# A two-feed-forward, one-attention layer on one core: three stages put into one block, attention's weights prepared beside the others

## The chip, the core and the metric

The kernel runs on one core of one Trainium2 chip. A core has TensorE (PE), VectorE (DVE), ScalarE (ACT), GpSimd (POOL) and SyncE (SP), each with its own instruction stream, tied together by semaphores, and 16 DMA engines. The metric is the device time of one launch in microseconds (us), the lower the better.

## The reference

`x` has shape 16 x 1024 x 256. The layer is a feed-forward with its weights and inputs quantized to 4 bits, a causal linear attention with 16 heads, and the same feed-forward once more. LayerNorm stands in front of each.

```python
def _L0_attn_ref(x, Wqkv, bqkv, Wout, bout, gamma, beta):
    qkv = x @ Wqkv.T + bqkv
    q, k, v = jnp.split(qkv, 3, axis=-1)            # 16 heads of 16
    q = (jax.nn.elu(q) + 1.0 + FEAT_EPS) / jnp.sqrt(jnp.asarray(E, q.dtype))
    k = jax.nn.elu(k) + 1.0 + FEAT_EPS
    kv_cumsum = jnp.cumsum(jnp.einsum('blhe,blhf->blhef', k, v), axis=1)
    num = jnp.einsum('blhe,blhef->blhf', q, kv_cumsum)
    den = jnp.einsum('blhe,blhe->blh', q, jnp.cumsum(k, axis=1))[..., None] + FEAT_EPS
    out = (num / den).reshape(B, L, D) @ Wout.T + bout
    return (out - mu) / jnp.sqrt(var + LN_EPS) * gamma + beta

def _L0_ffn_ref(x, w_gate, w_up, w_down):           # fp4_linear quantizes x and w by blocks of 16
    h = jax.nn.silu(fp4_linear(x, w_gate)) * fp4_linear(x, w_up)
    return fp4_linear(h, w_down)

x = x + 0.5 * _L0_ffn_ref(_layernorm(x, axis=-1), L0_ffn_w_gate, L0_ffn_w_up, L0_ffn_w_down)
x = x + _L0_attn_ref(_layernorm(x, axis=-1), L0_attn_Wqkv, ...)
x = x + 0.5 * _L0_ffn_ref(_layernorm(x, axis=-1), L0_ffn_w_gate, L0_ffn_w_up, L0_ffn_w_down)
```

## The kernel before

The input is cut into N = 128 tiles of 128 rows (partitions) by 256. All of them stay in on-chip memory, in `x_sb`, from the first load to the last store. The program is a row of five blocks, each of which every engine leaves before any engine enters the next: `prepare_ffn` (quantized weights, L141), `ffn` for half 0 (L306), `prepare_attention` (L1012), `attention` (L602), `ffn` for half 1.

Inside a stage each engine runs a `step(i)` of its own, called by `pipeline` (L85): some first steps written out, a hardware loop of 8 steps a turn (4 in attention), some last steps written out. Engines work on different tiles in one step: in the feed-forward, ScalarE normalizes tile i+5, GpSimd makes the two-part input `x_hl` of tile i+2 (L503, L507), SyncE turns it by a transposing DMA into `xT` (L403), TensorE multiplies tile i by gate and up (L577), VectorE makes `hx` (L429) and its block scales (L436 to L480), GpSimd makes `h_hl` of tile i-2 (L512, L513), SyncE turns it into `hT` (L409), TensorE multiplies tile i-4 by down (L587) and VectorE adds it to `x_sb` (L456, semaphore `added`). In attention the chain of a tile is: statistics (L757), `rstd` and `shift` on GpSimd (L833 to L857), `xn` and `x_hl` (L911 to L866), `xT` (L731), queries, keys and values (L946, L953), `expo` (L898, L900, then L784 on VectorE, semaphore `feat`), scores (L983, L798), states (L804, L807, L840, L780), numerator (L967, L973), `o` (L793), `oT` (L737), output projection into `ps_z` (L1005), its LayerNorm (L752 to L862, L766, semaphore `attn_added`).

The order on each engine is the order of the code. SyncE issues every DMA of the kernel: its queue holds the loads of x (L391, each of which waits for the one before it to land), both kinds of transposes and the stores. SyncE's `pipeline` in the feed-forward starts 14 steps ahead, so that the loads of tiles 0 to 12 stand in front of the first `xT`.

`prepare_attention` loads the weights, folds biases in, finds a power-of-two scale (`partition_all_reduce` on GpSimd, L1069), splits the weights into two 16-bit parts `qkvo_hi` and `qkvo_lo` on VectorE (L1139 to L1141) and turns them by 32 TensorE transposes (L1156) and ScalarE copies (L1169).

## Time and profile before

| | us |
|---|---|
| median of 3 runs | 2363.45 (2363.09 to 2365.65) |
| the profiled execution, its own time | 2364.28 |
| its span in the trace | 2362.6 |
| TensorE, VectorE busy | 2174.2 (92%), 2134.8 (90%) |
| ScalarE, GpSimd busy | 1857.8 (79%), 1970.0 (83%) |

A row of the view in order of time reads: start, length, engine, line, operation, what it writes and reads, and in brackets how long the engine sat idle before it and what ended that. "SPq" is SyncE issuing a DMA, not the transfer itself. "issue" means idle time that no other engine's work explains. PEclk is the share of full speed that TensorE's clock was granted: 1.00 stands for 2.4 GHz, 0.50 for 1.2 GHz.

### The profile page before, as it was taken

The numbers are of one execution on the slowest core, as the hardware profiler recorded it, in microseconds if no ns is written. First come the engines' busy times: TensorE is split into PE (matmuls) and PEld (weight loads), VectorE is DVE, ScalarE is ACT, GpSimd is POOL, SyncE is SP. The second block draws the span as 40 slices with busy tenths as digits, with TensorE's granted clock in tenths as the row PEclk, the third lists the DMA queues.
The fourth block names the chain that finished last, engine by engine and source line by source line (L and its number), as shares of the span: only waits on it lengthen the run. The fifth ranks groups of instructions, "written<-read, shape, count | busy, mean of one in ns | idle before, by whom it ended". The sixth has DMA issues, their size and how long they took to land. (4 is left out here: it accounts for less than half of the span.)

```text
span 2362.6 us, 84983 instructions
## 1 busy us (share of the span) xinstructions
PE 2174.2 (92%) x27394; PEld 1559.3 (66%) x27394; DVE 2134.8 (90%) x5243; ACT 1857.8 (79%) x3910; POOL 1970.0 (83%) x3237
## 2 busy tenths in 40 slices
PE   1499999999999469999999999996999999999998
PEld 1266666666666358898989898983556656656565
DVE  7499999999999649999999999996999999999997
ACT  2588888888888267888888888885888888888885
POOL 0499999999999358999999999995988998988996
PEclk9799999999999779999999999997999999999999
DMA  1265555555555313333333333331555555555555
GB/s 37 71 117 114 113 111 115 116 114 114 114 112 95 72 39 69 68 68 68 68 68 68 68 68 68 68 68 29 104 113 114 109 115 112 109 116 110 111 114 117
DMA packets 729026, 215.24 MB, mean 91 GB/s; under 512 B 660358, under 2 KB 728710, under 8 KB 728966
## 3 DMA queue, kind: packets, MB, share of 16 engines
q1 hardware_dynamic: 728966, 214.52, 44.6%
q8 instruction: 28, 0.46, 0.1%
q14 instruction: 32, 0.26, 0.0%
HBM read 20.38 MB, written 16.78 MB: 16 GB/s over the span
## 5 line engine op out<-in xcount | busy, mean ns | idle before, releaser
L577 PE MATMUL ffn_ps_gu<-wgu_hi,ffn_xT 128*128 128x512 f16 (+1 forms) x3072 | 737.4, 363 | 50.4 <-DMA ffn_xT<-ffn_x_hl 50.4
L577 PEld LDWEIGHTS ffn_ps_gu<-wgu_hi,ffn_xT 128*128 128x128 f16 x3072 | 300.4, 98 | 336.2 <-DMA ffn_xT<-ffn_x_hl 52.7
L577 PE MATMUL ffn_ps_gu<-wgu_lo,ffn_xT 128*128 128x512 f16 (+1 forms) x1536 | 431.3, 363 | 0.0
L531 ACT ACTIVATE ffn_quarter<-ffn_y,offsets 128x960 int16<-128x960 f32 (+2 forms) x264 | 282.7, 1071 | 186.6 <-DVE ffn_y L467 186.0
L587 PE MATMUL ffn_ps_down<-wd_hi,ffn_hT 128*128 128x256 f16 x2816 | 351.2, 274 | 24.2 <-DVE x_sb L456 15.9
L512 POOL TENSOR_TENSOR ffn_h_hl<-ffn_q,ffn_h_scale_hi 128x704 f16<-128x704 f16 x256 | 350.8, 1370 | 15.9 <-DVE ffn_h_scale_lo L473 13.2
L513 POOL TENSOR_TENSOR ffn_h_hl<-ffn_q,ffn_h_scale_lo 128x704 f16<-128x704 f16 x256 | 353.8, 1382 | 0.0
L436 DVE TENSOR_REDUCE ffn_per_block<-ffn_hx 128x60 f32<-128x960 f32 (+2 forms) x264 | 298.5, 1131 | 42.2 <-ACT ffn_hx L561 19.8
L587 PEld LDWEIGHTS ffn_ps_down<-wd_hi,ffn_hT 128*128 128x128 f16 x2816 | 264.8, 98 | 106.7 <-issue 35.2
L467 DVE TENSOR_TENSOR ffn_y<-ffn_hx,ffn_per_block 128x960 f32<-128x960 f32 (+2 forms) x264 | 295.2, 1118 | 0.0
L559 ACT ACTIVATE ffn_odd<-ffn_quarter,offsets 128x960 f16<-128x960 int16 (+2 forms) x264 | 278.6, 1055 | 0.0
L429 DVE SCALAR_TENSOR_TENSOR ffn_hx<-ffn_ps_gu,unscale,ffn_silu 128x704 f32<-128x704 f32 x256 | 243.4, 951 | 37.1 <-PE ffn_ps_gu L577 24.4
L577 PEld LDWEIGHTS ffn_ps_gu<-wgu_lo,ffn_xT 128*128 128x128 f16 x1536 | 150.3, 98 | 155.2 <-issue 1.8
L526 ACT ACTIVATE ffn_silu<-ffn_ps_gu,unscale 128x704 f32<-128x704 f32 x256 | 211.8, 828 | 36.0 <-PE ffn_ps_gu L577 36.0
L503 POOL TENSOR_TENSOR ffn_x_hl<-ffn_q,ffn_x_scale_hi 128x256 f16<-128x256 f16 x256 | 157.5, 615 | 82.1 <-POOL ffn_rstd L495 40.4
L587 PE MATMUL ffn_ps_down<-wd_lo,ffn_hT 128*128 128x256 f16 x1536 | 210.6, 274 | 0.0
L946 PE MATMUL attn_ps_qk<-attn_xT,attn_wqkv_hi 128*128 128x128 f16 x2048 | 180.3, 221 | 15.9 <-DMA attn_xT<-attn_x_hl 15.9
L495 POOL TENSOR_TENSOR ffn_rstd<-ffn_rstd,minus_half 128x1 f32<-128x1 f32 x256 | 168.2, 657 | 20.0
L507 POOL TENSOR_TENSOR ffn_x_hl<-ffn_q,ffn_x_scale_lo 128x256 f16<-128x256 f16 x256 | 159.9, 625 | 20.0
L587 PEld LDWEIGHTS ffn_ps_down<-wd_lo,ffn_hT 128*128 128x128 f16 x1536 | 150.5, 98 | 18.1
L798 DVE TENSOR_TENSOR attn_scores<-attn_ps_sc,attn_causal 128x1024 f32<-128x1024 f32 x128 | 155.5, 1215 | 0.1
L946 PEld LDWEIGHTS attn_ps_qk<-attn_xT,attn_wqkv_hi 128*128 128x128 f16 x2048 | 142.5, 98 | 17.6 <-issue 16.2
(202 smaller groups left out, 5375.4 us busy)
## 6 DMA issues: line engine op xcount, KB each, us to landing
attn_v_eo<-attn_v_nat SPq DMA_DIRECT2D x512, 34.0 KB, 1.9
x_sb<-in_L_attn_x SPq DMA_DIRECT2D x128, 128.0 KB, 2.3
out<-x_sb SPq DMA_DIRECT2D x128, 128.0 KB, 2.1
ffn_xT<-ffn_x_hl SPq DMA_TRANSPOSE x256, 2.4
ffn_hT<-ffn_h_hl SPq DMA_TRANSPOSE x256, 3.6
attn_xT<-attn_x_hl SPq DMA_TRANSPOSE x128
attn_oT<-attn_o_hl SPq DMA_TRANSPOSE x128, 2.4
raw_qkvo<-in_L_attn_Wqkv SPq DMA_DIRECT2D x1, 768.0 KB, 5.1
```

The lines of the kernel that those rows point to most:

```text
L429: nc.vector.scalar_tensor_tensor(hx[par][:, 0:INNER], ps_gu[par][:, INNER:2 * INNER], unscale[:, 1:2], silu[:], ALU.mult, ALU.mult).then_i ...
L436: nc.vector.tensor_reduce(amax[:, blocks_in(front)], blocks(hx[par][:, front]), AXX, ALU.max, apply_absolute_value=True).then_inc(S["amax" ...
L467: nc.vector.tensor_tensor(blocks(y[:, front]), blocks(hx[par][:, front]), over_block(inv[:, at], at.stop - at.start), ALU.mult).then_inc(S ...
L495: nc.gpsimd.tensor_tensor(rstd[oth][:], rstd[oth][:], minus_half[:], ALU.pow).then_inc(S["rstd"], 1)
L512: nc.gpsimd.tensor_tensor(blocks(h_hl[par][:, 0:INNER]), blocks(q[par][:, 0:INNER]), over_block(h_scale_hi[par][:], HB), ALU.mult)
L513: nc.gpsimd.tensor_tensor(blocks(h_hl[par][:, INNER:]), blocks(q[par][:, 0:INNER]), over_block(h_scale_lo[par][:], HB), ALU.mult).then_inc ...
L526: nc.scalar.activation(silu[:], ps_gu[par][:, 0:INNER], ACT.Silu, scale=unscale[:, 0:1]).then_inc(S["silu"], 1)
L531: nc.scalar.activation(quarter[:, back], y[:, back], ACT.Identity, bias=offsets[:, 0:1], scale=4.0 / HALF_MIN).then_inc(S["quarter"], 1)
L559: nc.scalar.activation(odd[:, back], quarter[:, back], ACT.Identity, bias=offsets[:, 1:2], scale=HALF_MIN / 4.0).then_inc(S["odd"], 1)
L577: last = nc.tensor.matmul(ps_gu[par][:, a:b], xT[par][:, c, :], w[:, k, a:b], start=(n == 0), stop=(n == len(terms) - 1))
L587: last = nc.tensor.matmul(ps_down[:, 0:D], hT[par][:, c, :], w[:, c, :], start=(n == 0), stop=(n == len(terms) - 1))
L946: last = nc.tensor.matmul(ps_qk[:, col, :], w[:, at], aT, start=(n == 0), stop=(n == len(terms) - 1))
```

## The change

The five blocks become one, and no engine waits for all others between stages. A new `stages` writes each engine's whole program: feed-forward 0's first steps and loop, then 8 turns in which the last 8 steps of feed-forward 0 alternate with the first 8 of attention, attention's loop, then 7 turns in which the last 7 steps of attention alternate with the first 7 of feed-forward 1.

```diff
+    for i in range(first, end):
+        step(eng, i, i % 2)
+
+
+def in_turns(eng, step, first, end, turn):
+
     with eng.Fori(first, end - turn + 1, turn) as i:
         for k in range(turn):
-            step(i + k, (first + k) % 2)
-    for i in range(end, n + behind):
-        step(i, i % 2)
+            step(eng, i + k, (first + k) % 2)
+
+
+def stages(eng, N, ffn_0, attn, ffn_1, ffn_ahead=6, between=None):
+
+    first, ahead = 6, 4
+
+    def loop_end(n_ahead, begin, turn):
+        return begin + (N - n_ahead - begin) // turn * turn
+
+    in_order(eng, ffn_0, -ffn_ahead, first)
+    if between:
+        between(eng)
+    in_turns(eng, ffn_0, first, loop_end(ffn_ahead, first, TURN), TURN)
+    in_order(eng, ffn_0, loop_end(ffn_ahead, first, TURN), N + first - 2 * ahead)
+    for k in range(2 * ahead):
+        ffn_0(eng, N + first - 2 * ahead + k, k % 2)
+        attn(eng, k - ahead, k % 2)
+    attn_end = loop_end(ahead, ahead, ATTN_TURN)
+    in_turns(eng, attn, ahead, attn_end, ATTN_TURN)
+    in_order(eng, attn, attn_end, N + ahead - 7)
+    for k in range(7):
+        attn(eng, N + ahead - 7 + k, (N + ahead - 7 + k) % 2)
+        ffn_1(eng, k - 6, k % 2)
+    in_order(eng, ffn_1, 1, first)
+    in_turns(eng, ffn_1, first, loop_end(6, first, TURN), TURN)
+    in_order(eng, ffn_1, loop_end(6, first, TURN), N + first)
 
 
 def macaron(nc, x, wqkv, bqkv, wout, bout, gamma, beta, wg, wu, wd, out):
```

Attention's weights are prepared right after the feed-forward's, before any stage. In their preparation GpSimd subtracts the last column and makes the low part, and both parts are turned by two transposing DMAs of SyncE between step 5 and the loop of feed-forward 0. The rows of V's weights and biases are loaded by 16 small DMAs in the order in which they are used. The turned weights lie as `w_hi`, `w_lo` of [128, 8, 2, 128], so the V and output matmuls read 256 columns as two pieces of 128.

```diff
+        def _(sp):
+            def weights_turned(sp):
+                of_ffn.turn(sp)
+                of_attn.turn(sp)
+
+            of_ffn.sync(sp)
+            of_attn.sync(sp)
+            stages(sp, N, of_ffn_0.sync, of_attn_steps.sync, of_ffn_1.sync, 14, weights_turned)
...
+            stages(pe, N, of_ffn_0.tensor, of_attn_steps.tensor, of_ffn_1.tensor)
+
+
+@dataclass
+class Programs:
+
+    sync: Callable = None
+    turn: Callable = None
+    vector: Callable = None
+    gpsimd: Callable = None
+    scalar: Callable = None
+    tensor: Callable = None
+    reduce: Callable = None
+
+
+def prepare_ffn(nc, sem, scratch, wg, wu, wd, wgu_hi, wgu_lo, wd_hi, wd_lo, unscale, ident, ident16, minus_half, eps, minus_one, offsets):
 
     NG = WT * XB
     ND = DC * HB
     with ExitStack() as scope:
-        def sb(name, shape, dt=F32):
...
+
+    def sync(sp):
+        sp.dma_start(raw[:, 0:2 * DC, :], wqkv[0:2 * D].rearrange("(t p) k -> p t k", p=P)).then_inc(loaded, 16)
+        sp.dma_start(raw[:, QT:, :], wout.rearrange("(t p) k -> p t k", p=P)).then_inc(loaded, 16)
+        sp.dma_start(bias[:, 0:2 * DC], bqkv[0:2 * D].rearrange("(t p) -> p t", p=P), allow_slow_non_contiguous=True).then_inc(loaded, 16)
+        for j in range(HEADS // 2):
+
+            pair_of = slice(2 * D + j * 2 * E, 2 * D + (j + 1) * 2 * E)
+            sp.dma_start(raw[j * E:(j + 1) * E, 2 * DC:QT, :], wqkv[pair_of].rearrange("(a e) k -> e a k", a=2)).then_inc(loaded, 16)
+            sp.dma_start(bias[j * E:(j + 1) * E, 2 * DC:QT], bqkv[pair_of].rearrange("(a e) -> e a", a=2), allow_slow_non_contiguous=True).then_inc(loaded, 16)
+        for j, v in enumerate((bout, gamma, beta)):
+            sp.dma_start(rows[:, j, :], v.unsqueeze(0).to_broadcast([P, D])).then_inc(loaded, 16)
+
+    def turn(sp):
+        sp.wait_ge(split, 1)
+        for part, dst in ((hi, A.w_hi), (lo, A.w_lo)):
+            sp.dma_start_transpose(dst[:].rearrange("p t c m -> p (t c) m"), part).then_inc(S["w_turned"], 16)
+        sp.wait_ge(S["w_turned"], 32)
...
+                                pattern=[[0, DC], [E, 2 * PAIRS]], channel_multiplier=-1).then_inc(diag_ready, 1)
+        nc.gpsimd.memset(keep[:].rearrange("p (b c) -> p b c", c=CH)[:, :, 0:1], 0.0).then_inc(done, 1)
+
+
+        pool.wait_ge(loaded, 16 * LOADS)
+        nc.gpsimd.tensor_tensor(raw[:, 0:QT, 0:D - 1], raw[:, 0:QT, 0:D - 1], raw[:, 0:QT, D - 1:D].to_broadcast([P, QT, D - 1]), ALU.subtract).then_inc(centred, 1)
+        pool.wait_ge(centred, 1)
+        nc.gpsimd.tensor_scalar(raw[:, 0:2 * DC, D - 1], bias[:, 0:2 * DC], 1.0, None, ALU.add).then_inc(with_bias, 1)
+        nc.gpsimd.tensor_scalar(raw[:, 2 * DC:QT, D - 1], bias[:, 2 * DC:QT], 0.0, None, ALU.add).then_inc(with_bias, 1)
+
+    def reduce(pool):
+        pool.wait_ge(top_ready, 1)
+        nc.gpsimd.partition_all_reduce(gtop, top, P, RMAX).then_inc(gtop_ready, 1)
+        pool.wait_ge(scaled, 1)
+        nc.gpsimd.tensor_tensor(lo, raw_all, hi, ALU.subtract).then_inc(split, 1)
```

All scratch of the preparations lies in tiles 38 and up of `x_sb`, and the three stages' buffers lie at addresses written by hand in one area that they share. Where the barrier kept a stage from overwriting the one before, there are now single waits at the first steps. In feed-forward 1:

```diff
+
+                if half == 1 and isinstance(tm, int) and tm == 0:
+                    for even_odd in ("_even", "_odd"):
+                        act.wait_ge(T["xT" + even_odd], N * 8)
+                if half == 0:
+                    act.wait_ge(x_loaded, (tm + 1) * 16)
+                else:
+                    act.wait_ge(attn_added, tm + 1)
...
+
+                if half == 1 and isinstance(tn, int) and tn < 2:
+                    act.wait_ge(T["v_done"], N)
+                    act.wait_ge(T["k_odd"], N + tn - 1)
+                ready(act, "shift", tn)
...
+
+                if half == 1 and isinstance(tg, int) and tg == 1:
+                    pe.wait_ge(T["kv_first"], N)
+                    pe.wait_ge(T["o_ready"], N)
...
+
+                if half == 1 and isinstance(td, int) and td == 0:
+                    pe.wait_ge(T["z_gamma"], N)
```

and in attention (`F` is the feed-forward's semaphores):

```diff
+                freed(dve, "mid", i, 1)
+                if isinstance(i, int) and i == 0:
+                    last_turned(dve, "hT")
...
+            if isinstance(i, int) and i == -2:
+
+                pool.wait_ge(F["q"], N + X_AHEAD)
+                for j in range(2):
+                    nc.gpsimd.memset(v_nat[j][:], 1.0).then_inc(set_up, 1)
+                    nc.gpsimd.memset(v_eo[j][:], 0.0).then_inc(set_up, 1)
+            if isinstance(i, int) and i == 1:
+                last_turned(pool, "hT")
+                nc.gpsimd.memset(before[0][:], 0.0).then_inc(set_up, 1)
+                pool.wait_ge(set_up, 5)
...
+                freed(act, "kv_done", i, 1)
+                if isinstance(i, int) and i == 0:
+                    act.wait_ge(F["h_split"], N)
...
+
+                if isinstance(tf, int) and tf == 0:
+                    act.wait_ge(S["consts"], CONSTS)
+                    act.wait_ge(F["q"], N + X_AHEAD)
...
+
+                if isinstance(tf, int) and tf == 0:
+                    pe.wait_ge(S["consts"], CONSTS)
+                    pe.wait_ge(S["w_turned"], 32)
+                    pe.wait_ge(F["h"], N)
+                turned(pe, "xT", tf, oth)
+                freed(pe, "feat", tf, 1)
...
+
+                if valid(i, N):
+                    ready(pe, "k_nat", i)
+                for n, (aT, w, k) in enumerate(terms):
+                    last = nc.tensor.matmul(ps_v.rearrange("p (t m) -> p t m", t=DC), aT, w[:, 2 * DC:QT, k], start=(n == 0), stop=(n == len(terms) - 1))
+                last.then_inc(S["v_done"], 1)
+            if valid(tn, N):
+
+                if isinstance(tn, int) and tn == 0:
+                    pe.wait_ge(F["added"], N)
```

How this moves instructions. SyncE at the start of the program; `x_sb` as a target of weights is scratch. Before, the x loads stood behind a barrier:

```order
L189 DMA x_sb<-in_L_ffn_w_down 128x2x704
L145 UNCONDITIONAL_BRANCH
L385 UNCONDITIONAL_BRANCH [waits barrier_Pool_Activation_PE_DVE_SP_release]
L391 DMA x_sb<-in_L_attn_x 128x256
L391 DMA x_sb<-in_L_attn_x 128x256 [waits x_loaded] x12
L403 DMA_TRANSPOSE ffn_xT<-ffn_x_hl 128x4x128 [waits ffn_x_split]
L391 DMA x_sb<-in_L_attn_x 128x256 [waits x_loaded]
```

Now they stand right behind the weights' own loads (rows 4 to 22 are loads of attention's weights and biases, of which the last two of the 16 small ones are shown):

```order
L1174 DMA x_sb<-in_L_attn_Wqkv 16x2x256
L1175 DMA x_sb<-in_L_attn_bqkv 16x2x1
L1177 DMA attn_rows<-in_L_attn_bout 128x256
L1177 DMA attn_rows<-in_L_attn_gamma 128x256
L1177 DMA attn_rows<-in_L_attn_beta 128x256
L495 DMA x_sb<-in_L_attn_x 128x256
L495 DMA x_sb<-in_L_attn_x 128x256 [waits x_loaded] x12
L507 DMA_TRANSPOSE ffn_xT_88<-ffn_x_hl_84 128x4x128 [waits ffn_x_split]
L495 DMA x_sb<-in_L_attn_x 128x256 [waits x_loaded]
```

The 13 x loads no longer wait for the preparation to end, and they still stand in front of the first transpose.

SyncE at the loop of feed-forward 0. Before:

```order
L391 DMA x_sb<-in_L_attn_x 128x256 [waits x_loaded]
L403 DMA_TRANSPOSE ffn_xT<-ffn_x_hl 128x4x128 [waits ffn_x_split,ffn_up_done]
L409 DMA_TRANSPOSE ffn_hT<-ffn_h_hl 128x11x128 [waits ffn_h_split,ffn_down_done]
L92 UNCONDITIONAL_BRANCH
L92 ISA
L391 ISA [waits x_loaded]
L391 DMA x_sb<-in_L_attn_x 128x256
```

Now:

```order
L495 DMA x_sb<-in_L_attn_x 128x256 [waits x_loaded]
L507 DMA_TRANSPOSE ffn_xT_89<-ffn_x_hl_85 128x4x128 [waits ffn_x_split,ffn_up_done]
L513 DMA_TRANSPOSE ffn_hT_91<-ffn_h_hl_87 128x11x128 [waits ffn_h_split,ffn_down_done]
L1182 DMA_TRANSPOSE attn_w_hi<-x_sb 128x16x128 [waits qkv_split,prep_copied]
L1182 DMA_TRANSPOSE attn_w_lo<-x_sb 128x16x128
L96 UNCONDITIONAL_BRANCH [waits attn_w_turned]
L96 ISA
L495 ISA [waits x_loaded]
L495 DMA x_sb<-in_L_attn_x 128x256
```

Two transposes of 16 squares of 128 x 128 each, and a wait for both to land, have come in front of the loop's first load and transposes.

GpSimd at the start of attention. `ISA` with no operands stands where the program sets something up for the next kind of GpSimd instruction. Before:

```order
L820 MEMSET attn_v_eo 128x544
L817 MEMSET attn_x_hl 128x1
L818 MEMSET attn_x_hl 128x1
L819 MEMSET attn_v_nat 128x272
L820 MEMSET attn_v_eo 128x544
L833 ISA
L833 TENSOR_TENSOR attn_rstd<-attn_mv,eps 128x1 [waits attn_stats,attn_set_up]
L847 TENSOR_TENSOR attn_rstd<-attn_rstd,minus_half 128x1 [waits attn_var]
L857 TENSOR_SCALAR attn_shift<-attn_mv,attn_rstd 128x1 [waits attn_rstd]
L866 TENSOR_TENSOR attn_x_hl<-attn_xn,attn_x_hl 128x255 [waits attn_x_hi]
```

Now, where feed-forward 0 ends; `ffn_h_hl_86` and `_87` are tiles 126 and 127:

```order
L975 TENSOR_SCALAR attn_shift_140<-attn_mv_136,attn_rstd_138 128x1 [waits attn_rstd]
L984 TENSOR_TENSOR attn_x_hl_143<-attn_xn,attn_x_hl_143 128x255 [waits attn_x_hi]
L608 TENSOR_TENSOR ffn_h_hl_86<-ffn_q_68,ffn_h_scale_hi_74 128x704 [waits ffn_hT_even,ffn_h_scale_lo,ffn_q]
L609 TENSOR_TENSOR ffn_h_hl_86<-ffn_q_68,ffn_h_scale_lo_76 128x704
L932 MEMSET attn_v_nat_156 128x272 [waits ffn_q]
L933 MEMSET attn_v_eo_158 128x544
L932 MEMSET attn_v_nat_157 128x272
L933 MEMSET attn_v_eo_159 128x544
L951 TENSOR_TENSOR attn_rstd_139<-attn_mv_137,eps 128x1 [waits attn_stats]
L965 TENSOR_TENSOR attn_rstd_139<-attn_rstd_139,minus_half 128x1 [waits attn_var]
L975 TENSOR_SCALAR attn_shift_141<-attn_mv_137,attn_rstd_139 128x1 [waits attn_rstd]
L984 TENSOR_TENSOR attn_x_hl_144<-attn_xn,attn_x_hl_144 128x255 [waits attn_x_hi]
```

The work on attention's first tiles has moved in between the feed-forward's last products, and the `ISA` row is gone from here; it stands once, in the preparation, behind the second `partition_all_reduce` and in front of the subtraction that makes the low part.

## Rows read from the trace of the kernel before

**Rows 1.** Stretches: length, busy us (instructions) of each engine, clock, DMA share, GB/s.

```profile
0.00:95.00 95.00, 14.12 (x120) 10.66 (x121) 50.45 (x73) 31.17 (x59) 11.58 (x40) 0.84 0.19 47
95.00:784.00 689.00, 683.84 (x4374) 423.98 (x4373) 653.45 (x1640) 588.63 (x1243) 622.65 (x867) 1.00 0.56 111
784.00:862.00 78.00, 29.79 (x318) 22.58 (x315) 30.59 (x75) 23.27 (x66) 21.15 (x49) 0.67 0.19 42
862.00:1604.00 742.00, 729.75 (x17857) 663.06 (x17848) 703.36 (x1739) 603.60 (x1249) 665.50 (x1369) 1.00 0.33 68
1604.00:1643.00 39.00, 17.86 (x300) 11.24 (x290) 20.50 (x61) 18.40 (x50) 19.54 (x43) 0.69 0.11 22
```

**Rows 2.** Order of time, start: begin us, length, engine, line, what, [idle before].

```profile
51.36 1.61 DVE L247 TENSOR_TENSOR lo_down<-x_sb,hi_down 128x1408 f16<-128x1408 f32 x1
...
59.74 26.87 SPq L391 DMA_DIRECT2D x_sb<-in_L_attn_x  x13
...
67.48 0.18 POOL L493 TENSOR_TENSOR ffn_rstd<-ffn_var,eps 128x1 f32<-128x1 f32 x1 [34.54 <-ACT ffn_squares L551]
...
74.35 0.62 POOL L507 TENSOR_TENSOR ffn_x_hl<-ffn_q,ffn_x_scale_lo 128x256 f16<-128x256 f16 x1
...
86.80 1.31 SPq L403 DMA_TRANSPOSE ffn_xT<-ffn_x_hl  x1
...
89.36 1.89 PE L577 MATMUL ffn_ps_gu<-wgu_hi,ffn_xT 128*128 128x512 f16 x4 [31.50 <-DMA ffn_xT<-ffn_x_hl]
```

**Rows 3.** Order of time: end of feed-forward 0, attention's weights.

```profile
784.40 0.95 DVE L429 SCALAR_TENSOR_TENSOR ffn_hx<-ffn_ps_gu,unscale,ffn_silu 128x704 f32<-128x704 f32 x1 [0.92 <-PE ffn_ps_gu L577]
...
812.80 2.35 DVE L1090 TENSOR_REDUCE qkvo_top<-raw_qkvo 128x1 f32<-128x1536 f32 x2
...
823.80 1.76 DVE L1141 TENSOR_TENSOR qkvo_lo<-raw_qkvo,qkvo_hi 128x1536 f16<-128x1536 f32 x1
...
826.45 0.69 DVE L1141 TENSOR_TENSOR qkvo_lo<-raw_qkvo,qkvo_hi 128x512 f16<-128x512 f32 x1
```

**Rows 4.** Groups by shape: count | busy us, mean ns | idle us before.

```profile
L870 POOL TENSOR_TENSOR attn_o_hl<-attn_o,attn_o_hl 128x256 f16<-128x256 f32 x128 | 86.3, 674 | 5.4 <-ACT attn_o_hl L918 5.3
...
L493 POOL TENSOR_TENSOR ffn_rstd<-ffn_var,eps 128x1 f32<-128x1 f32 x256 | 48.7, 190 | 53.2 <-ACT ffn_squares L551 53.0
```

**Rows 5.** SyncE's queue in order of time, feed-forward 0's first steps.

```profile
123.48 1.39 SPq L409 DMA_TRANSPOSE ffn_hT<-ffn_h_hl  x1
```

**Rows 6.** The page's part 6: DMA issues, last number median us to landing.

```profile
ffn_xT<-ffn_x_hl SPq DMA_TRANSPOSE x256, 2.4
ffn_hT<-ffn_h_hl SPq DMA_TRANSPOSE x256, 3.6
```

**Rows 7.** TensorE in order of time: tile 8's gate and up matmuls begin.

```profile
131.28 1.03 PE L577 MATMUL ffn_ps_gu<-wgu_hi,ffn_xT 128*128 128x512 f16 x4
```

**Rows 8.** All engines in order of time, attention's start.

```profile
840.92 0.18 POOL L833 TENSOR_TENSOR attn_rstd<-attn_mv,eps 128x1 f32<-128x1 f32 x1 [7.03 <-issue]
...
852.20 0.75 DVE L784 SCALAR_TENSOR_TENSOR attn_expo<-attn_ps_qk,attn_unscale,attn_expo 128x512 f32<-128x512 f32 x1 [6.29 <-ACT attn_expo L900]
...
862.25 0.75 DVE L784 SCALAR_TENSOR_TENSOR attn_expo<-attn_ps_qk,attn_unscale,attn_expo 128x512 f32<-128x512 f32 x1 [1.09 <-ACT attn_expo L900]
```

**Rows 9.** VectorE in order of time, end of attention, feed-forward 1's start.

```profile
1604.54 0.75 DVE L784 SCALAR_TENSOR_TENSOR attn_expo<-attn_ps_qk,attn_unscale,attn_expo 128x512 f32<-128x512 f32 x1 [0.83 <-ACT attn_expo L900]
...
1642.53 0.95 DVE L429 SCALAR_TENSOR_TENSOR ffn_hx<-ffn_ps_gu,unscale,ffn_silu 128x704 f32<-128x704 f32 x1 [5.80 <-PE ffn_ps_gu L577]
```

**Rows 10.** TensorE, the same stretch.

```profile
1619.92 0.40 PE L1002 MATMUL attn_ps_z<-attn_bout,attn_ones 128*128 128x256 bf16 x1 [4.14 <-DMA attn_oT<-attn_o_hl]
...
1635.80 1.89 PE L577 MATMUL ffn_ps_gu<-wgu_hi,ffn_xT 128*128 128x512 f16 x4 [14.21 <-DMA ffn_xT<-ffn_x_hl]
```

**Rows 11.** Groups by shape, TensorE.

```profile
L953 PE MATMUL attn_ps_kT_v<-attn_wqkv_hi,attn_xT 128*128 128x256 f16 x512 | 77.6, 275 | 0.0
```

1274 lines of the change are left out of this document (618 added, 656 removed).

## The prediction

> **What bounds the kernel now.** I read the table of stretches first [rows 1], which cuts the span where VectorE or TensorE goes from one stage to the next. In a loop VectorE and TensorE are both nearly full: in feed-forward 0's stretch TensorE is busy 683.84 of 689 us and VectorE 653.45, in attention's 729.75 and 703.36 of 742. Nothing that the change moves can shorten those. The other three stretches are nearly empty. From 0 to 95 us TensorE works 14.12 us and VectorE 50.45. From 784 to 862 they work 29.79 and 30.59 of 78 us. From 1604 to 1643 they work 17.86 and 20.50 of 39. TensorE's granted clock in the last two is 0.67 and 0.69, between its levels of 1.2 and 2.4 GHz, against 1.00 in the loops. The reader should see 212 us of span in which the time is a chain of waits. Then I read these stretches in order of time, to find which wait ends last in each, and what the new order puts in its place. The profiled execution took 2364.28 us, 0.83 above the median, and its span was 2362.6.
>
> **Term 1, the start.** Now, VectorE ends its preparation at 52.97 (51.36 + 1.61); the barrier opens, and SyncE's 13 x loads, each waiting for the one before, run from 59.74 to 86.61, 2.07 us each. The first transpose is behind them and goes at 86.80, although its input was ready at 74.35 + 0.62 = 74.97. TensorE begins at 89.36 [rows 2]. After the change the x loads stand behind the weights' own loads. I estimate those 25 issues at 0.5 us each, since nothing in front of them waits for a computation; so the x loads run from about 14 to 41 us, up to 49 if each is slowed by the weights' traffic, all beside VectorE's preparation. They drop off the path.
> What is late next is GpSimd. VectorE's preparation gets longer: attention's weights took it from 812.80 to 827.14, less 1.76 + 0.69 for the low parts that GpSimd now makes [rows 3], so 11.9 us, and it is free at about 65. It had waited there anyway. The low part is 2048 columns on GpSimd. Its rows give 674 ns for 256 columns and 190 ns for one column [rows 4], or 1.9 ns a column and 4.1 us in all. In front of it stands the `ISA` step. The nearest row is the 7.03 us that GpSimd sat idle for no other engine before its first `attn_rstd` at 840.92, and that idle stands exactly where the `ISA` is [rows 8]. From the second reduction at about 55.8 this gives 62.8, and the subtraction ends at 66.9. That is 0.6 earlier than GpSimd's first feed-forward instruction today, at 67.48 [rows 2]. So x_split(0) comes at 74.4, and with 2.6 us from the transpose's issue to the matmul (86.80 to 89.36, rows 2), TensorE begins at 77.0: a gain of 12.4. GpSimd's centring of 1530 columns (2.9 us by the same price) falls while it is idle.
> Against it stands SyncE's hold. Before the loop it issues two transposes of 16 blocks and waits for both. The transposes of 4 and 11 blocks land in 2.4 and 3.6 us [rows 6]: 0.17 us a block, so 4.5 us for 16, and 2.7 more for the second behind it. They start when SyncE has issued the hT of the last first step, 124.87 [rows 5], and end at 132.1; then a load and the xT of tile 8, which lands at about 135.1. TensorE wanted it at 131.28 [rows 7], so it is 3.8 late. VectorE has about 1.5 us in hand there, which leaves 2.3. Bounds: nothing if the weights' transposes run beside the rest, 7.2 if the whole hold counts. **Term 1 is 12.4 - 2.3 = 10, between 5 and 13.**
> The hold is where I weighed a rule. Rows 6 amount to 229 KB moved in 1.2 us of extra landing time, 191 GB/s. The Trainium skill (DMA: Bandwidth & Descriptors, Latency and other measured facts) gives 261 GB/s effective for a transpose with a non-contiguous middle dimension. By that rate the two would need an estimated 5.7 us instead of 7.2, and the term would be 11.5. I stay with the rows.
>
> **Term 2, feed-forward 0 to attention.** Now, `hx` of the last tile starts at 784.40, attention's weights are reduced, split and turned, and GpSimd pays the 7.03 us [rows 3, 8]. The first `expo` in the form that VectorE finishes is at 852.20, the third at 862.25 [rows 8]. All of the preparation is gone from here. I walked the new order engine by engine with the durations of these same instructions. xT(0) is issued about 789.8 and lands at 792.2 (2.4, rows 6); queries and keys end at about 796; ScalarE's table load (it stays) and its two exponentials end at 799; so expo(0) is at 799.0, 53.2 earlier. Then the turns cost. GpSimd has h_hl(127) between attention's inputs, its hT lands 3.6 us later, near 803.4, and down(127) stands in TensorE's row in front of attention's second values. That puts expo(1) near 805.2 and expo(2) near 811.9, against 862.25. **Term 2 is 50.4.** From expo(2) on nothing of the feed-forward is left on TensorE, so I let the normal period start there. Bounds: 53, if only expo(0) counts; 45, if one tile more comes a full period of 5.8 us late (742 us for 128 tiles, rows 1).
>
> **Term 3, attention to feed-forward 1.** Now the last `expo` is at 1604.54, the last output projection starts at 1619.92, and gate and up of tile 0 start only at 1635.80, with `hx` at 1642.53 [rows 9, 10]. In the new order x_hl(0) of the feed-forward stands behind the LayerNorm of z of tile 126 on GpSimd, and VectorE's first scales stand in front of o(127). In my walk x_split(0) is done near 1626.7, xT(0) lands 2.4 later and gate and up start at 1629.3, 6.5 us earlier. Here I am least sure. If the last projection alone gated feed-forward 1, gate and up would follow it by some 3 us, at 1623: 12.8. If the turns push o(127) back twice as far as I think (2.8 us in my walk), it is about 3. **Term 3 is 6.5, between 3 and 13.** The LayerNorm statistics of tile 0 need only tile 0's end, and are long ready.
>
> **What else changes** is free. The V and output matmuls read 256 columns as two pieces of 128 contiguous ones; addresses and banks move; and 13 loads of x share DMA engines with weights that were loaded anyway. The steps in the three loops are otherwise the same instructions in the same order, so the periods stay.
>
> **Sum.** 10 + 50.4 + 6.5 = 66.9; 2364.28 - 66.9 = 2297.4 for the profiled execution, and 0.8 less by the median. I say 2297. The bounds add to gains of 53 and 79: 2311 and 2285.
>
> **Rivals.**
> *The turns overlap better than I walk* (chance 0.10). For: every engine has over 50% idle in both stretches [rows 1]. Against: the order on each engine is fixed. It needs the upper bounds of all three terms and a little more, a gain of 82: 2282.
> *The turns collide* (0.12). There are 8 + 7 turns, in each of which an engine stops for the late item of one stage while the other stage's item is ready. If 8 of the 15 each pay one landing of 2.4 us [rows 6] in series, 19 us are lost: 2316. For it: TensorE's clock falls in stretches with waits, and a matmul of 128x512 x4 is 1.89 us at the start against 1.03 in the loop [rows 2, 7].
> *The x loads don't come early* (0.03), because a wait or a DMA queue keeps them behind the preparation. Term 1 is gone: 2307.
> *Slower than before* (0.03). The moving operand in two pieces costs TensorE a second start. A tile has 12 such matmuls, 1536 in all, and they take 77.6 / 512 = 0.152 us each now [rows 11]. If the time doubled, that is 233 us, of which TensorE's 12 us of slack in attention [rows 1] hide little: 2297 + 221 = 2518. It decides from 67 us on, that is 0.52 us a tile, or 0.04 us a matmul beyond the slack. Against: both pieces are contiguous runs of 128, and the queries' and keys' matmuls already stream 128 at a time.
>
> **How the numbers follow.** The forecast has 0.72. Its bounds give the range, 2284 to 2311, which takes in the start rival and about half of the better overlap, and leaves out collision, slower, and the rest: about 0.8 held. A measurement of this kernel can tell 0.2%, 4.7 us, from no change. Faster by more: 0.95. Within it, 0.02, for two pieces that cost about 0.04 us a matmul. Slower, 0.03, the last rival.
>
> **What would show it.** TensorE's first gate and up near 77 instead of 89.4; the 13 x loads ended before 50; two weight transposes of SyncE near 125 to 132 with one stall of TensorE of 2 to 4 us; from the last `hx` of feed-forward 0 to the first `expo` some 15 us instead of 67.8, to the third 27.5 instead of 77.9; from the last `expo` to feed-forward 1's first `hx` about 31.5 instead of 38.0; the V group's mean still near 275 ns; the loops' periods equal within 0.02 us a step. Wrong would be the whole if a loop's period moved by 0.05 us (6 us a stage), or if a wait of a first step turned out to hold an engine past the end of the other stage.

## The result, and the profile after

| | before | changed |
|---|---|---|
| median, us | 2363.27 (4 runs, 2362.72 to 2365.65) | 2303.88 (4 runs, 2301.66 to 2305.78) |
| the profiled execution's span | 2362.6 | 2301.4 |
| TensorE, VectorE busy | 92%, 90% | 94%, 93% |

The ratio is 0.9746, with a 95% interval from 0.973 to 0.9763: 59.4 us faster, where the forecast was 66 and its range 2284 to 2311. The table of stretches of the changed kernel, which answers to [rows 1] (length, then busy us and instructions of PE, PEld, DVE, ACT and POOL, the granted clock, DMA share, GB/s):

```profile
0.00:87.00 87.00, 14.91 (x123) 10.95 (x124) 68.09 (x108) 31.53 (x61) 24.14 (x56) 0.88 0.27 68
87.00:780.00 693.00, 683.74 (x4368) 425.19 (x4367) 653.50 (x1640) 589.49 (x1241) 622.39 (x867) 1.00 0.55 112
780.00:809.00 29.00, 21.99 (x291) 18.41 (x290) 14.91 (x35) 18.20 (x35) 20.34 (x39) 0.94 0.40 72
809.00:1551.00 742.00, 729.56 (x17865) 663.07 (x17867) 703.07 (x1739) 603.73 (x1251) 663.71 (x1364) 1.00 0.32 68
1551.00:1583.00 32.00, 18.26 (x284) 12.02 (x269) 19.16 (x61) 16.86 (x44) 20.77 (x45) 0.73 0.17 29
```

The two empty stretches between stages were 78 and 39 us, and are 29 and 32. The start is still 87 us long. VectorE has 68.09 us of work in it where it had 50.45, since attention's weights lie there now. The engines have the same work in the loops as before (TensorE 683.74 and 729.56 us, where it had 683.84 and 729.75), and attention's stretch is as long; feed-forward 0's is 693 us and not 689, because SyncE's hold at its start, which comes below, falls into it.

To see where each us went I cut both traces at the same instructions, VectorE's `hx` of a tile of a feed-forward and its `expo` of a tile of attention. All numbers are differences of start times:

| stretch | before | changed | gain | forecast |
|---|---|---|---|---|
| 0 to hx(0), feed-forward 0 | 94.51 | 85.87 | 8.64 | 12.4 |
| hx(0) to hx(16) | 85.80 | 90.85 | -5.05 | -2.3 |
| hx(16) to hx(127) | 604.09 | 604.46 | -0.37 | 0 |
| hx(127) to expo(0) | 67.80 | 14.04 | 53.76 | 53.2 |
| expo(0) to expo(2) | 10.05 | 13.79 | -3.74 | -2.8 |
| expo(2) to expo(120) | 699.56 | 700.58 | -1.02 | 0 |
| expo(120) to hx(0), feed-forward 1 | 80.72 | 73.67 | 7.05 | 6.5 |
| hx(0) to the last VectorE instruction | 717.34 | 715.39 | 1.95 | 0 |
| sum | 2359.87 | 2298.65 | 61.22 | 67 |

The forecast's column adds the parts of its walk. Both stage boundaries came out as walked. The start gave 3.6 us where 10 were forecast; these 6.5 us are the miss, and the other rows together are 0.7 us above their forecast. Rows of the changed kernel's start in order of time, all engines (start, length, engine, line, what, idle before):

```profile
19.37 27.09 SPq L495 DMA_DIRECT2D x_sb<-in_L_attn_x  x13
...
22.87 2.74 POOL L1207 TENSOR_TENSOR x_sb<-x_sb 128x1530 f32<-128x1530 f32 x1 [18.99 <-DMA attn_rows<-in_L_attn_beta]
23.14 4.61 DVE L309 SCALAR_TENSOR_TENSOR x_sb<-x_sb 88x2048 f32<-88x2048 f32 x1
...
57.82 0.37 POOL L1214 PARTITION_ALL_REDUCE x_sb<-x_sb  x1 [22.39 <-DVE x_sb L1230]
...
65.01 4.04 POOL L1216 TENSOR_TENSOR x_sb<-x_sb 128x2048 f16<-128x2048 f32 x1 [6.82 <-issue]
65.09 4.11 DVE L1272 CAST x_sb<-x_sb 3x256 bf16<-3x256 f32 x1
...
76.31 0.62 POOL L603 TENSOR_TENSOR ffn_x_hl<-ffn_q,ffn_x_scale_lo 128x256 f16<-128x256 f16 x1
...
77.11 1.32 SPq L507 DMA_TRANSPOSE ffn_xT<-ffn_x_hl  x1
```

The x loads are off the path, as forecast, though 5 us later than the walk had them: 19.37 to 46.46, and not 14 to 41. VectorE's scaling of `w_up` at 23.14 takes 4.61 us; the same instruction took 2.29 before. GpSimd's centring runs at 22.87, beside it. From there on VectorE is 2.5 us behind its times in the kernel before, so GpSimd's second reduction starts at 57.82, not 55.8. Then the idle time called issue (6.82 us), and the low part. A second VectorE instruction is stretched beside that: a conversion of 3 x 256 takes 4.11 us.

SyncE's queue around the loop's start, then TensorE's first matmul and VectorE's `hx` of tile 8 with their idle times:

```profile
116.37 2.20 SPq L1182 DMA_TRANSPOSE attn_w_hi<-x_sb  x1
118.62 3.12 SPq L1182 DMA_TRANSPOSE attn_w_lo<-x_sb  x1
123.97 0.37 SPq L495 DMA_DIRECT2D x_sb<-in_L_attn_x  x1
```

```profile
127.38 1.08 PE L676 MATMUL ffn_ps_gu<-wgu_hi,ffn_xT 128*128 128x512 f16 x4 [4.55 <-DMA ffn_xT<-ffn_x_hl]
...
132.83 0.95 DVE L528 SCALAR_TENSOR_TENSOR ffn_hx<-ffn_ps_gu,unscale,ffn_silu 128x704 f32<-128x704 f32 x1 [4.53 <-PE ffn_ps_gu L676]
```

The hold is 116.37 to 123.97. TensorE stands idle 4.55 us for xT(8), and VectorE 4.53 us in front of `hx` of tile 8.

### The profile page after: what moved, and what is told of

It is laid out like the page before. It is cut to its first block, busy times and chain, and to the rows that moved or that the text cites. A ratio compares the mean times of both kernels' runs of the same rounds, so it can differ in the third digit from the quotient of the medians.

```text
span 2301.4 us, 84889 instructions
## 1 busy us (share of the span) xinstructions
PE 2168.6 (94%) x27362; PEld 1558.6 (68%) x27362; DVE 2135.8 (93%) x5237; ACT 1853.5 (81%) x3878; POOL 1981.5 (86%) x3241
## 4 chain that ended last, share of the span: by engine, by line
PE 39%; DVE 37%; issue 9%; POOL 8%; DVEq 2%; DMA 1%; SPq 1%; ACT 1%; POOLq 0%; ACTq 0%
DVE ffn_y L566 10%; DVE ffn_per_block L535 8%; PE attn_ps_qk L1068 7%; DVE ffn_hx L528 6%; PE ffn_ps_gu L676 6%; PE attn_ps_sc L1107 6%; POOL ffn_h_hl L609 3%; PE attn_ps_z L1129 3%; DVE ffn_q L562 3%; PE ffn_ps_down L688 3%; PE attn_ps_kT_v L1075 3%; PE attn_ps_num L1091 3%; PE attn_ps_num L1097 3%; POOL ffn_h_hl L608 3%; PE attn_ps_kv L1119 2%
## 5 line engine op out<-in xcount | busy, mean ns | idle before, releaser
L608 POOL TENSOR_TENSOR ffn_h_hl<-ffn_q,ffn_h_scale_hi 128x704 f16<-128x704 f16 x256 | 351.2, 1372 | 13.8 <-issue 6.3
L566 DVE TENSOR_TENSOR ffn_y<-ffn_hx,ffn_per_block 128x960 f32<-128x960 f32 (+2 forms) x264 | 295.4, 1119 | 0.0
L599 POOL TENSOR_TENSOR ffn_x_hl<-ffn_q,ffn_x_scale_hi 128x256 f16<-128x256 f16 x256 | 157.8, 616 | 69.8 <-POOL ffn_rstd L591 40.3
L1068 PE MATMUL attn_ps_qk<-attn_xT,attn_w_hi 128*128 128x128 f16 x2048 | 178.1, 219 | 0.0
L688 PEld LDWEIGHTS ffn_ps_down<-wd_lo,ffn_hT 128*128 128x128 f16 x1536 | 150.6, 98 | 17.7
L660 ACT ACTIVATE ffn_hx<-x_sb,ffn_shift,ffn_rstd 128x256 f32 (+1 forms) x256 | 149.9, 585 | 8.7 <-POOL ffn_shift L601 8.7
```

Source lines behind the costliest of these rows:

```text
L566: nc.vector.tensor_tensor(blocks(y[:, front]), blocks(hx[par][:, front]), over_block(inv[:, at], at.stop - at.start), ALU.mult).then_inc(S ...
L608: nc.gpsimd.tensor_tensor(blocks(h_hl[par][:, 0:INNER]), blocks(q[par][:, 0:INNER]), over_block(h_scale_hi[par][:], HB), ALU.mult)
L688: last = nc.tensor.matmul(ps_down[:, 0:D], hT[par][:, c, :], w[:, c, :], start=(n == 0), stop=(n == len(terms) - 1))
L1068: last = nc.tensor.matmul(ps_qk[:, col, :], w[:, col, k], aT, start=(n == 0), stop=(n == len(terms) - 1))
```

## Experiments

The cuts of code are shortened. Ratios are to runs of the kernel before on the same chip. A time with "1 run" carries no verdict: a single run can't be told from the changed kernel's unless it is several us away (experiment 9).

**1. The hold alone: the weights' transposes in front of the first xT.**

```diff
-    in_order(eng, ffn_0, -ffn_ahead, first)
     if between:
+        in_order(eng, ffn_0, -ffn_ahead, -2)
+        turn_first(eng)
+        in_order(eng, ffn_0, -2, first)
         between(eng)
...
             def weights_turned(sp):
                 of_ffn.turn(sp)
-                of_attn.turn(sp)
+                sp.wait_ge(attn_sems["w_turned"], 32)
```

Here `turn_first` issues the two transposes without a wait for their landing, and `between` has the wait for both.

> The changed kernel, with SyncE's two transposes of attention's weights issued behind the x load of tile 11, in front of the first xT, instead of between step 5 and the loop; the wait for them to land stays in front of the loop. In the changed kernel the first hx starts at 85.87 us and the ninth at 132.83, 46.96 later; before the change it was 42.05. Theory 'the hold': SyncE's 7.6 us (116.37 to 123.97) make this difference. Then the distance comes down to about 42.1, TensorE's idle 4.55 us at 127.38 is gone, the first hx moves by less than 0.5 us (the low part is ready at 69.05, two transposes take until 76.7, and the first xT goes at 77.11 anyway), and the time falls by 4.5 to 5 us, to about 2299. Rival 'the catch-up': the loop starts late because stages that had slack before lost it when the start came earlier; then the distance stays over 45 and the time changes by under 1 us.

2295.15 us (2292.84 to 2296.79, 4 runs), ratio 0.9708 (0.9691 to 0.9724). SyncE in its trace:

```profile
68.69 2.03 SPq L1186 DMA_TRANSPOSE attn_w_hi<-x_sb  x1
70.78 2.38 SPq L1186 DMA_TRANSPOSE attn_w_lo<-x_sb  x1
```

hx(0) to hx(8) takes 42.08 us, where the changed kernel takes 46.96 and the kernel before 42.05. The hold was the whole difference, 4.9 us, and in front of the first xT it costs nothing: hx(0) starts at 85.60. The median is 8.7 us below the changed kernel's first runs and 6.1 below its later ones (experiment 9), more than 4.9 in both cases; experiment 9 says where most of the rest lies.

**2. Who stretches VectorE's instruction.** GpSimd's subtraction is cut to one column, so that attention's weights aren't centred.

```diff
-nc.gpsimd.tensor_tensor(raw[:, 0:QT, 0:D - 1], raw[:, 0:QT, 0:D - 1], raw[:, 0:QT, D - 1:D].to_broadcast(...), ALU.subtract)
+nc.gpsimd.tensor_tensor(raw[:, 0:QT, 0:1], raw[:, 0:QT, 0:1], raw[:, 0:QT, D - 1:D], ALU.subtract)
```

> The changed kernel, with GpSimd's subtraction of the last column (1530 columns, 2.74 us at 22.87) cut to one column, which leaves attention's weights uncentred. In the changed kernel VectorE's scaling of w_up at 23.14 takes 4.61 us, where the same instruction took 2.29 before the change. Theory 'GpSimd slows VectorE': the two run at the same time and share a path to memory; then the instruction takes 2.29 again, everything on VectorE behind it and the first hx come 2.3 us earlier (83.5), and so does the end. Rival 'the DMA traffic': the loads of attention's weights and of x, which were not there before, slow it; then it stays over 4 us and the first hx stays at 85.9.

```profile
23.12 0.21 POOL L1207 TENSOR_TENSOR x_sb<-x_sb 128x6 f32<-128x6 f32 x1 [19.23 <-DMA attn_rows<-in_L_attn_beta]
23.43 0.27 POOL L1209 TENSOR_SCALAR x_sb<-x_sb 128x4 f32<-128x4 f32 x1
23.65 2.29 DVE L309 SCALAR_TENSOR_TENSOR x_sb<-x_sb 88x2048 f32<-88x2048 f32 x1
23.66 2.37 POOL L1210 TENSOR_SCALAR x_sb<-x_sb 128x2 f32<-128x2 f32 x1
```

VectorE's instruction takes 2.29 us, with the loads running as before. It is GpSimd. The row behind it shows the other side: VectorE was first now, by 0.01 us, and GpSimd's addition of two columns, a matter of 0.3 us (the row above it has four columns), takes 2.37, as long as VectorE is at work to within 0.1. In the changed kernel it went to and fro: behind the centring GpSimd's addition of four columns, 0.27 us here, took 2.15 from 25.70 on, while VectorE finished its scaling. Whichever starts first has the path, and the other stands. The Trainium skill (GPSIMD Engine Reference, Specifications) says that the two share interfaces to SBUF, with contention where VectorE's instruction has two SBUF inputs, as this one has, or runs in a mode that takes two ports; the Trainium skill (SBUF — State Buffer, SBUF: two separate sides) adds that the first to start keeps the pair of interfaces for the whole instruction. By these rows that holds here. It was a rule against this change, and the prediction didn't weigh it. Not every pair is held up: in the feed-forward's loops VectorE's `ffn_y` product (L566), of whose two inputs one lies in PSUM, takes 1.15 us at 202.09, and GpSimd's product L599 runs inside it, from 202.30 on, in 0.61 us. Their means over the whole kernel are 1.149 and 0.616 us, so neither is stretched.

The second part of the theory fell. The reduction came 1.83 us earlier, at 55.99, but `hx(0)` only 0.28. The idle time in front of the low part was 7.72 us this time, 0.9 more, and TensorE ran tile 0 at its lower clock for longer: its first four groups of matmuls took 1.86, 1.06, 1.91 and 0.97 us, where they had 1.86, 1.06, 1.47 and 0.59 (experiment 7 is on this). The time was 2300.49 us (1 run), not told from the changed kernel's.

**3. The low part on VectorE again.**

```diff
-        pool.wait_ge(scaled, 1)
-        nc.gpsimd.tensor_tensor(lo, raw_all, hi, ALU.subtract).then_inc(split, 1)
...
-        nc.vector.tensor_copy(hi, raw_all).then_inc(scaled, 1)
+        then(nc.vector.tensor_copy(hi, raw_all))
+        nc.vector.tensor_tensor(lo, raw_all, hi, ALU.subtract).then_inc(split, 1)
```

> The changed kernel, with attention's low part made by VectorE (as before the change, 2.45 us) and not by GpSimd (4.04 us from 65.01). Theory 'the step in front of the subtraction belongs to GpSimd's change from the reduction to any ordinary instruction, and the subtraction blocks VectorE': GpSimd is idle for 6.8 us between its reduction at 57.8 and its first ffn_rstd, which starts at about 65 instead of 69.0; VectorE's conversion of 3 x 256 at 65.09 takes 0.28 and not 4.11; VectorE is free at 71.0 - 3.8 + 2.4 = 69.6, and the first hx comes 1.5 us earlier, 84.3. Rival 'it belongs to the subtraction': ffn_rstd starts as soon as the statistics are there, at about 64. Rival 'VectorE isn't blocked': the conversion still takes 4 us, VectorE is free at 73.5, and the first hx comes 2 us later.

2301.61 us (1 run), not told from the changed kernel's. GpSimd's first `ffn_rstd`, and VectorE's conversion:

```profile
65.37 0.18 POOL L589 TENSOR_TENSOR ffn_rstd<-ffn_var,eps 128x1 f32<-128x1 f32 x1 [7.20 <-issue]
...
67.40 0.28 DVE L1271 CAST x_sb<-x_sb 3x256 bf16<-3x256 f32 x1
```

All three numbers as the first theory had them: GpSimd idle for 7.20 us behind the reduction, now in front of `ffn_rstd`; the conversion 0.28 us; `hx(0)` at 84.28. So the 4.04 us on GpSimd cost VectorE 3.8 us as well, while VectorE does it in 2.3.

**4. No turns.** The stages follow one another on each engine, without barriers.

```diff
-    for k in range(2 * ahead):
-        ffn_0(eng, N + first - 2 * ahead + k, k % 2)
-        attn(eng, k - ahead, k % 2)
+    in_order(eng, ffn_0, N + first - 2 * ahead, N + first)
+    in_order(eng, attn, -ahead, ahead)
...
-    in_order(eng, attn, attn_end, N + ahead - 7)
-    for k in range(7):
-        attn(eng, N + ahead - 7 + k, (N + ahead - 7 + k) % 2)
-        ffn_1(eng, k - 6, k % 2)
-    in_order(eng, ffn_1, 1, first)
+    in_order(eng, attn, attn_end, N + ahead)
+    in_order(eng, ffn_1, -6, first)
```

> The changed kernel without the turns: on every engine feed-forward 0's last step stands in front of attention's first, and attention's last in front of feed-forward 1's first; still one block without barriers. In the changed kernel the last hx of feed-forward 0 to the third expo takes 27.8 us (before the change 77.9), and the last expo to feed-forward 1's first hx 31.5 (before 38.0). Theory 'moving the weights gave nearly all, the turns a little': the third expo comes some 33 us after the last hx, because TensorE's queries stand behind the last down product (17.8 us after the last hx before the change), and the second distance is about 35, since the barrier itself cost little; the time is 2304 + 5 + 3.5 = 2312. Rival 'the turns cost as much as they give': both distances stay within 1.5 us of the changed kernel's, 2304. Rival 'the turns are the gain': the third expo comes 45 us or more after the last hx.

2318.82 us (1 run), 15 to 18 more than the two medians of the changed kernel. hx(127) to expo(2) takes 38.46 us (27.83 with turns, 77.85 before), and the last expo to hx(0) of feed-forward 1 35.68 (31.52, and 38.0 before). Of the 50 us of the first boundary the moved weights and the missing barriers give 39.4 and the turns 10.6 (12.2 by the second trace of the changed kernel, experiment 9); I had said 5. At the second boundary the turns give 4.2 us, or 5.9 by the second trace. The rows say why:

```profile
798.59 0.48 DVE L550 SCALAR_TENSOR_TENSOR x_sb<-ffn_ps_down,ffn_h_unscale,x_sb 128x256 f32<-128x256 f32 x1 [2.40 <-PE ffn_ps_down L683]
...
799.44 0.18 DVE L878 BATCH_NORM_AGGREGATE attn_mv<-attn_bn 128x2 f32<-128x6 f32 x1
799.70 0.19 POOL L946 TENSOR_TENSOR attn_rstd<-attn_mv,eps 128x1 f32<-128x1 f32 x1 [6.76 <-DVE attn_mv L878]
...
805.35 0.58 PE L1063 MATMUL attn_ps_qk<-attn_xT,attn_w_hi 128*128 128x128 f16 x4 [6.80 <-DMA attn_xT<-attn_x_hl]
...
810.94 0.75 DVE L892 SCALAR_TENSOR_TENSOR attn_expo<-attn_ps_qk,attn_unscale,attn_expo 128x512 f32<-128x512 f32 x1 [4.79 <-ACT attn_expo L1015]
```

I had put TensorE's queue last. It is VectorE's. Attention's first statistics (L865, L878) stand behind the feed-forward's last addition to x (L550) there, so GpSimd's `rstd` waits until 799.70 with everything behind it; TensorE has been idle 6.80 us when the queries come.

**5. The x loads late again.** SyncE waits for the low part (`attn_split[0]`) before the first x load.

```diff
             of_attn.sync(sp)
+            sp.wait_ge(attn_split[0], 1)
             stages(sp, N, ...)
```

> The changed kernel, with SyncE waiting for attention's low part (69.05 us) before the first x load; this takes the early x loads back and leaves all else. 13 loads of 2.07 us then stand in front of the first xT, as before the change: it goes at about 69.1 + 27 = 96.2 instead of 77.11, and the first hx comes at about 104.5 instead of 85.87, 18.6 us later; the time is 2322. Rival: loads that share the DMA engines with nothing run faster, 1.6 us each, and the first hx comes at 98.

2322.0 us (1 run), 18.1 more than the changed kernel's first median and 20.8 more than its second, and hx(0) at 103.53, 17.7 us later. The loads ran from 68.94 to 94.35 in 1.95 us each, a little faster than beside the preparation. The early loads are worth about 18 us of this kernel. The table shows 8.64 at the start, since the longer preparation took the rest.

**6. Both reductions together.** VectorE finds the maxima of attention's weights before it waits for the feed-forward's scale.

```diff
+            top_of_attn(dve)
             dve.wait_ge(gtop_ready, 1)
...
+    def top_of_weights(dve):
+        dve.wait_ge(with_bias, 2)
+        for w, at in enumerate(parts):
+            last = nc.vector.tensor_reduce(top[:, w:w + 1], raw_all[:, at], AXX, ALU.max, apply_absolute_value=True)
+        last.then_inc(top_ready, 1)
```

> The changed kernel, with VectorE's maxima of attention's weights in front of its wait for the feed-forward's scale, so that GpSimd runs its two reductions close together. In the changed kernel the second starts at 57.82, GpSimd then sits idle for 6.82 us, and the low part (4.04) ends at 69.05, where ffn_rstd starts. Theory 'the 7 us follow the last reduction': they now pass while VectorE works; GpSimd waits only for VectorE's high part (62.6), the subtraction ends at about 66.7, the first x_hl is ready 2.3 us earlier than 76.93, at 74.6, and the first hx between 83.5 and 85.5, the later the longer TensorE stays at its lower clock. Rival 'they come in front of any subtraction of that size': the subtraction still starts 6.8 us after its operands are ready, at 69, and the first x_hl is ready at 81.

```profile
43.78 0.37 POOL L1217 PARTITION_ALL_REDUCE x_sb<-x_sb  x1 [8.37 <-DVE x_sb L1224]
62.74 4.06 POOL L1219 TENSOR_TENSOR x_sb<-x_sb 128x2048 f16<-128x2048 f32 x1 [18.59 <-DVE x_sb L1262]
```

```profile
78.91 1.87 PE L679 MATMUL ffn_ps_gu<-wgu_hi,ffn_xT 128*128 128x512 f16 x4 [16.64 <-DMA ffn_xT<-ffn_x_hl]
80.56 1.06 PE L679 MATMUL ffn_ps_gu<-wgu_lo,ffn_xT 128*128 128x512 f16 x2
81.42 1.91 PE L679 MATMUL ffn_ps_gu<-wgu_hi,ffn_xT 128*128 128x512 f16 x4
83.12 1.06 PE L679 MATMUL ffn_ps_gu<-wgu_lo,ffn_xT 128*128 128x512 f16 x2
```

With the last reduction at 43.78 the 7 us pass unseen, and the subtraction starts at 62.74, the moment that its operands are there. The first x_hl is ready 1.53 us earlier (75.40), and TensorE starts 1.53 earlier; then it works the first four groups of tile 0 at the lower clock (1.87, 1.06, 1.91, 1.06), and `hx(0)` is 0.43 us earlier, at 85.44. The time, 2303.84 (1 run), isn't told from the changed kernel's.

That it is the reduction which the 7 us follow is not shown, and the kernel before speaks against it:

```profile
815.28 0.42 POOL L1069 PARTITION_ALL_REDUCE qkvo_gtop<-qkvo_top  x1 [11.21 <-DVE qkvo_top L1090]
831.86 0.32 POOL L814 MEMSET attn_before<- 128x272 f32 x1 [16.16 <-POOLq L1015]
...
833.34 0.56 POOL L820 MEMSET attn_v_eo<- 128x544 f32 x1
840.92 0.18 POOL L833 TENSOR_TENSOR attn_rstd<-attn_mv,eps 128x1 f32<-128x1 f32 x1 [7.03 <-issue]
```

There 16.16 us and nine fills of memory stood behind the reduction, and the 7.03 us came all the same, in front of the first arithmetic instruction, where the `ISA` row stands. So time alone behind a reduction doesn't pay them. What both kernels have in common is the `ISA` step, behind the fills in the one and behind the last reduction in the other; in experiment 6 it must pass while GpSimd waits for the high part, since the subtraction starts as soon as that is there. That the step itself takes the 7 us is argued from its place and not shown. The Trainium skill (GPSIMD Engine Reference, Instruction dispatch) gives about 6 us, unseen in a profile, for the first call of a GpSimd routine whose code must be fetched; eight traces show 6.69 to 7.72 us between the last reduction and the next instruction, and the kernel before 7.03 us behind the fills. That this is such a fetch no run here shows.

**7. The clock.** 40 matmuls that nobody uses, between the preparation's last transpose and gate and up, on the kernel of experiment 1. Later 50 of them on the second combined version, which is in experiment 8.

```diff
+            for _ in range(WARM):
+                of_ffn_0.warm(pe)
             stages(pe, N, of_ffn_0.tensor, of_attn_steps.tensor, of_ffn_1.tensor)
...
+        def warm(pe):
+            nc.tensor.matmul(ps_gu[1][:, 0:512], wgu_hi[:, 0, 0:P], wgu_hi[:, 0, 0:512], start=True, stop=True)
```

> The kernel with the early turn, and 40 more matmuls of 128 x 512 on TensorE between the preparation's last transpose and the first gate and up, into a bank that the second tile overwrites; their results are not used. In the kernel with the early turn the first gate and up start at 79.96 after 20.12 us idle and take 1.87, 1.06, 1.68 and 0.59 us for the first four groups where the loop takes 1.03, 0.59, 1.03 and 0.59, and the first hx is at 85.60. Theory 'the clock': a TensorE that was at work is granted the higher clock at once; gate and up of tile 0 take about 4.1 us and not 6, and the first hx comes at 83.7. Rival 'the first matmuls are slow for their operands or their landing': the groups keep their durations and the first hx stays at 85.6. If 40 matmuls take more than the 20 us, the first hx comes later by what they stick out.

```profile
61.78 10.47 PE L700 MATMUL ffn_ps_gu<-wgu_hi 128*128 128x512 f16 x40 [2.02 <-ACT wd_lo L371]
80.59 1.89 PE L684 MATMUL ffn_ps_gu<-wgu_hi,ffn_xT 128*128 128x512 f16 x4 [8.34 <-DMA ffn_xT<-ffn_x_hl]
...
83.12 1.91 PE L684 MATMUL ffn_ps_gu<-wgu_hi,ffn_xT 128*128 128x512 f16 x4
```

2298.29 us (1 run). The 40 took 10.47 us and ended 8.34 us before gate and up. Those ran at the lower clock all the same, so this settled nothing. `hx(0)` came at 86.86 here; 0.6 of the 1.3 us against experiment 1 is a longer idle time behind the reduction (7.50 against 6.93).

> The same, with 50 idle matmuls of 128 x 512 on TensorE behind the preparation (12.6 us by the 10.47 us that 40 took; those 40 ended 8.3 us before the first gate and up, which then ran at the lower clock all the same). Theory 'the clock is granted to a TensorE that was at work just before': with at most 2 us between the last idle matmul and gate and up, tile 0 takes 4.1 us and not 6, and the first hx comes 1.5 to 1.9 us earlier than without them. Rival: the first groups are slow for another reason and stay at 1.86, 1.06 us.

```profile
64.36 10.96 PE L703 MATMUL ffn_ps_gu<-wgu_hi 128*128 128x512 f16 x50 [1.67 <-ACT wd_lo L374]
76.38 1.04 PE L687 MATMUL ffn_ps_gu<-wgu_hi,ffn_xT 128*128 128x512 f16 x4 [1.05 <-DMA ffn_xT<-ffn_x_hl]
77.25 0.59 PE L687 MATMUL ffn_ps_gu<-wgu_lo,ffn_xT 128*128 128x512 f16 x2
77.68 1.03 PE L687 MATMUL ffn_ps_gu<-wgu_hi,ffn_xT 128*128 128x512 f16 x4
78.55 0.59 PE L687 MATMUL ffn_ps_gu<-wgu_lo,ffn_xT 128*128 128x512 f16 x2
```

```profile
82.64 0.93 DVE L539 SCALAR_TENSOR_TENSOR ffn_hx<-ffn_ps_gu,unscale,ffn_silu 128x704 f32<-128x704 f32 x1
```

2293.30 us (2291.13 to 2299.80, 4 runs), ratio 0.9692 (0.9676 to 0.9708), not told from 2294.08 without the idle matmuls. With 1.05 us between the last idle matmul and gate and up, the four groups take 1.04, 0.59, 1.03 and 0.59 us, where they take 1.87, 1.06, 1.82 and 0.60 without. The clock was the cause of the long groups, and 2 us of TensorE's time are won. Both the number of idle matmuls and their distance changed between the two runs, so which of them did it isn't shown. But `hx(0)` stays at 82.64 (82.42 without), because VectorE is at the rows of attention's bias until then.

**8. Combined versions.** First: the reductions together, the low part on VectorE, and it and the bias's rows behind the x pieces of tiles 0 to 3; the high part turned in front of the first xT, the low part in front of step 1.

```diff
+            stages(sp, N, of_ffn_0.sync, of_attn_steps.sync, of_ffn_1.sync, 14, weights_turned, {-2: of_attn.turn[0], 1: of_attn.turn[1]})
...
+            stages(dve, N, of_ffn_0.vector, of_attn_steps.vector, of_ffn_1.vector, hooks={0: of_attn.rest})
```

> A version from what was found: the reductions together; the low part on VectorE again, and it and the bias's rows behind the x pieces of tiles 0 to 3, where VectorE waits for TensorE's first tile; the high part turned in front of the first xT and the low part in front of SyncE's step 1. I expect the first ffn_rstd near 63 (ScalarE's statistics are then the last input), VectorE's first pieces of x at 65.3, the first x_hl at 70.9 against 76.93 in the changed kernel, TensorE at 74.2, the first hx at 80.0 against 85.87, and from there to the ninth 42.1 to 43 against 46.96: 5.9 + 4.4 = 10.3 us, so a time of about 2293 from these, and about 2289 if the later stretches are as in the kernel with the early turn (2295.15), which had luck or a cause of its own there. Rival: the low part and the bias's rows (5.7 us) don't fit where VectorE waits, the first hx stays near 83, and the time near 2293.

2292.2 us (2291.01 to 2294.98, 4 runs), ratio 0.9693 (0.9673 to 0.9712). The first `ffn_rstd` came at 65.50 and not 63, for ScalarE's statistics: the maxima stood in front of the feed-forward's product, and ScalarE's first copy waits for that. Hence `hx(0)` at 82.72 and not 80.0, a miss; for the last 0.6 us it waited for VectorE's own rows of the bias, since ScalarE's `silu` of tile 0 was done at 82.11. From it to hx(8) 42.04 us.

> The combined version, with the maxima of attention's weights moved behind the feed-forward's last product and in front of its low parts, since in the combined version they stood 2.3 us in the way of ScalarE's first copy (its weights ended at 64.1 us where they had ended at 61.9). The second reduction then ends near 52 and the 7 us near 59, still in front of the first ffn_rstd. If ScalarE is what the first x_hl waits for, ffn_rstd starts at about 63.3 and not 65.50, x_hl is ready 2.2 us earlier than 73.09, and the first hx comes between 80.5 and 81.5, as TensorE's lower clock takes back part of it; the time is 2291 against 2292.2. If VectorE or GpSimd decides, nothing moves.

2294.08 us (2293.59 to 2296.22, 4 runs), ratio 0.9697 (0.9681 to 0.9714), and `hx(0)` at 82.42. A miss: `ffn_rstd` moved by 0.3 us, to 65.20, still behind ScalarE. The maxima now delayed the low parts of the feed-forward's weights, and with them TensorE's transposes and ScalarE's copies. Then, with the idle matmuls and the rows of the bias back in VectorE's idle 3.15 us:

> The second combined version with the idle matmuls, and the bias's rows back in front of the x pieces, where VectorE sat idle for 3.15 us (64.24 to 67.39); only the low part (2.29 us) stays where VectorE waits for TensorE. In the version before, silu of tile 0 was done at 80.03, but VectorE had the low part and the rows until 82.64 and started the first hx then. Theory 'VectorE's own queue held the first hx, which is why the higher clock bought nothing there': the first hx starts at 80.0 to 80.3 and everything to the ninth comes 2.4 us earlier, a time of about 2291. Rival: the rows don't fit before the x pieces, which start up to 0.3 us later, or another engine holds the first hx at over 82.

```profile
64.75 12.65 PE L703 MATMUL ffn_ps_gu<-wgu_hi 128*128 128x512 f16 x50 [2.02 <-ACT wd_lo L374]
...
76.94 2.29 DVE L1296 TENSOR_TENSOR x_sb<-x_sb 128x2048 f16<-128x2048 f32 x1
81.00 0.95 DVE L539 SCALAR_TENSOR_TENSOR ffn_hx<-ffn_ps_gu,unscale,ffn_silu 128x704 f32<-128x704 f32 x1 [1.77 <-PE ffn_ps_gu L687]
```

`hx(0)` starts at 81.00, after 1.77 us idle. VectorE had held it. It is still 0.7 us later than expected: the 50 idle matmuls took 12.65 us this time, where they had taken 10.96, and lay in the way of gate and up until 77.2.

2293.05 us (2291.4 to 2298.07, 5 runs), ratio 0.9700 (0.9687 to 0.9714), no less than the first combined version, whose start was 1.7 us later. In the traces those 1.7 us are lost again in attention: expo(2) to expo(120) takes 703.42 us here and 705.34 with the 50 idle matmuls before, where the other ten traces of kernels with turns have 699.5 to 701.3. Most of it is one distance, from expo(3) to expo(4), of 9.10 and 9.34 us where the others have 6.4 to 7.7. In both, SyncE takes 3.1 to 3.2 us to issue the four small copies of V there, where the traces of experiment 1 and of the first combined version have 2.38, and the transpose that TensorE waits for stands behind them; why SyncE is slower wasn't tried. The ratios of the four combined versions (0.9692 to 0.9700) and of experiment 1 (0.9708) lie inside one another's intervals: beyond the early turn, 4.6 us at the start bought nothing that the runs can tell.

**9. The changed kernel again**, to learn what repeats.

> The changed kernel once more, beside the others on one chip. It tells what of its distances repeats. In its first trace the third expo came 13.79 us after the first, at a granted clock of 0.95 (12.17 at 1.00 with the early turn), and feed-forward 1's first hx 31.52 after the last expo, at 0.76 (29.68 at 0.85). Theory 'chance': these differ from execution to execution, and the second trace has another value for at least one. Theory 'fixed by what went before': both repeat within 0.1 us. The time is 2303.9 within 2 us.

2301.23 us (2299.73 to 2304.16, 4 runs). Expo(0) to expo(2) takes 12.19 us, and the last expo to hx(0) 29.77. The same two stretches in the first trace of this kernel (the second one's row is in the table of the result), and in this one:

```profile
781.00:809.00 28.00, 20.99 (x284) 17.70 (x283) 14.45 (x33) 17.20 (x34) 19.34 (x39) 0.94 0.39 69
```

```profile
782.00:809.00 27.00, 19.98 (x289) 16.96 (x289) 14.58 (x34) 17.79 (x35) 19.52 (x39) 1.00 0.41 73
1552.00:1582.00 30.00, 15.57 (x254) 9.95 (x251) 19.25 (x61) 16.48 (x43) 20.07 (x44) 0.83 0.15 28
```

The same instructions, 1.6 and 1.8 us faster where the granted clock was 1.00 and 0.83 rather than 0.94 and 0.73. At the first place TensorE's rows account for it: between expo(0) and expo(2) the first trace has three groups of matmuls at the lower clock, which take 1.84, 1.12 and 1.86 us, and the second has the same at 1.16, 0.64 and 1.37, together 1.65 us. The first of the three:

```profile
800.34 1.84 PE L1107 MATMUL attn_ps_sc<-attn_q_rows,attn_k_eo 64*128 64x128 f32 x16 [0.86 <-POOL attn_k_eo L962]
```

```profile
801.78 1.16 PE L1107 MATMUL attn_ps_sc<-attn_q_rows,attn_k_eo 64*128 64x128 f32 x16 [0.86 <-POOL attn_k_eo L962]
```

So the clock differs from one execution of the same kernel to the next; in the twelve traces of kernels with turns the first distance was 12.2 or 13.8 us and the second 29.7 to 32.2. `hx(0)` at the start was 86.86 here against 85.87, as loads landed later (VectorE's scaling of `w_up` starts at 23.51, not 23.14) and the idle time behind the reduction was 7.26 us. The trace of experiment 1 had the good value at both, which is 3.5 of the 10.4 us between it and the first trace of the changed kernel; the hold gave 4.9, and the end behind the last `hx` 1.1, at a granted clock of 1.00 where the other has 0.91. One profile of a kernel can't tell an edit worth 2 us from this.

## Why the prediction was right, and where its sum was off

The range held the time, and the median was 7 us above the forecast. The mechanism was right at both boundaries; two parts of term 1 were mis-sized.

*What bounds it, and that the three empty stretches are chains of waits:* right. The loops gained -0.37, -1.02 and +1.95 us, 0.6 together. Feed-forward 1's loop runs 0.016 us a step faster (619.74 for 112 tiles against 621.57); it does so in all thirteen traces with one block (619.6 to 619.9), so the change did it, and why wasn't tried.

*Term 1, the start: the mis-sized term.* 10 forecast, 3.6 measured, below its lower bound of 5. Two steps of it failed, and the whole stayed in its range only because the other two terms held.
- "GpSimd's centring ... falls while it is idle." GpSimd was idle, VectorE was not, and 2.74 us of the one held the other for 2.3 (experiment 2), and 4.04 us of the low part held it for 3.8 (experiment 3). I asked whether the moved work had a free engine, not whether it had a free path to memory. The second reduction started 2.0 us after its forecast; without the centring it came 1.83 us earlier. With the reduction's own 0.37 us, which the walk left out, that is 2.1 of the 3.8 us by which `hx(0)` missed, as the idle time was 0.2 us shorter than forecast. The price of 1.9 ns a column (4.1 us against 4.04) and the 7.03 us (6.82) held. Of the rest, 0.4 is in the first tiles' chain; 0.2 in the issue; 0.8 from the issue of the first xT to TensorE's start, 3.33 us where it took 2.56 before and 2.70 in experiment 5 (these two had an x load that ended 0.2 us in front of the transpose; ten other traces without one have 3.15 to 3.41), and for that I have no cause; 0.3 is TensorE's lower clock in tile 0.
- "VectorE has about 1.5 us in hand there." It had none: its idle time in front of hx(8) was 4.53 us, TensorE's 4.55. The transposes took 7.6 us, near the 7.2 that the rows of the small ones gave; the other estimate, by the rate that the Trainium skill (DMA: Bandwidth & Descriptors, Latency and other measured facts) gives, was 5.7, and this trace does not bear it out. The step that failed is the slack: 1.5 us forecast, none measured. I had subtracted a lead that engines had in the old trace from a stall in the new one. The hold cost 4.9 us and not 2.3, and experiment 1 gave it all back.

*Term 2:* 50.4 forecast, 50.0 measured, and 51.6 in the second trace. The walk gave hx(127) to the first three expos as 14.6, 20.8 and 27.5; they came after 14.04, 20.16 and 27.83. The third agrees so well by chance of the clock: in the second trace it is 26.24. The walk was made instruction by instruction on each engine. Where I only guessed, in experiment 4, I was off by more than 5 us.

*Term 3:* last expo to hx(0) 31.5 forecast, 31.52 measured, but 29.77 in the second trace, so the agreement within 0.1 is luck. The size is right within the clock's step.

*The rivals:* the turns don't collide; experiment 4 shows them worth some 15 us. The x loads did come early. The two-piece operand costs nothing, as the group that answers to [rows 11] shows:

```profile
L1075 PE MATMUL attn_ps_kT_v<-attn_w_hi,attn_xT 128*128 128x256 f16 x512 | 76.8, 273 | 0.8 <-ACT attn_k_nat L1000 0.8
```

The mean is 273 ns, where it was 275.

## What to carry to other kernels

Work that moves to an idle engine is free only if no other engine shares what it uses there: look for an instruction that is suddenly twice as long in both engines' rows at the same time. Put a queue's long items where the queue's engine is idle (here SyncE issued nothing from 46.46 to 77.11, and the weights' parts were ready at 69.05), and count a hold in full, since a lead seen in an old trace isn't there for the new one. When stages are put end to end, walk each engine's order instruction by instruction; the late item was VectorE's statistics, not the matmuls that everybody watches.

## What the hardware showed that I had not expected

- GpSimd and VectorE can stop one another whole, in both directions: 2.29 us became 4.61, 0.28 became 4.11 and, the other way, 0.3 became 2.37. With one of VectorE's two inputs in PSUM, as in the loops, neither was stretched.
- Between the last `partition_all_reduce` and its next arithmetic instruction GpSimd is idle 6.7 to 7.7 us in one piece, also where fills of memory stand between them (7.03 us behind the fills in the kernel before); where it waits for VectorE there anyway, as in experiment 6, nobody pays for it.
- A start of TensorE 1.5 us earlier gave 0.43 in one pair of traces, since the first four groups of tile 0 then ran at the lower of its two clocks. 40 idle matmuls that ended 8.3 us ahead didn't help, and 50 that ended 1.05 us ahead did.
- The granted clock at a stage boundary differs from execution to execution of one kernel (0.94 or 1.00, 0.73 or 0.83), worth 1.6 and 1.8 us.
